# Dense passes of a two-layer attention and mixture kernel spread over three places, and layer 1's gates by tanh in pieces

## The chip, the cores and the metric

One core of a Trainium2 chip runs the whole program. The metric is the device time of one execution in microseconds. TensorE (PE) multiplies, VectorE (DVE), ScalarE (ACT) and GpSimd (POOL) do the rest; SyncE (SP) issues most of the DMAs and runs, as every engine does, its instructions in order.

## The reference

x is 16 sequences of 256 rows of 128 numbers (4096 rows, 32 tiles of 128 rows). Two layers follow each other:

```python
xn = layernorm(x);  s = attention0(xn);  g = silu(mixture0(xn));  x = x + s * g
xn = layernorm(x);  s = attention1(xn);  g = silu(mixture1(xn));  x = x + s * g
```

Attention 0 is softmax attention of 16 heads with a relative bias; attention 1 works over channels (8 heads of 16 by 16, RMS norm, l2-normalised q and k). Mixture 0 has 8 experts (128 to 512 to 128, exact gelu), top 2, plus half a shared expert, and a layer norm with gamma and beta. Mixture 1 has 4 experts and top 2 by a router with a hidden layer of 256:

```python
rh = gelu(x @ rW1 + rb1); probs = softmax(rh @ rW2 + rb2)
w, idx = top_k(probs, 2)
out = sum_e combine_w[e] * (gelu(x @ We1[e] + be1[e]) @ We2[e] + be2[e])
```

## The kernel before

Everything is fp32 but the scores' operands. The rows chosen for an expert are scattered to DRAM by POOL (`scatter_rows`), loaded as tiles of 256 rows, multiplied, and scattered back by POOL (`store_outputs`, L803) to `yg_dram`; the two choices of each row are then fetched by SP (`fetch`, L621) into `yy` and added by DVE (`add_choices`, L2122).

A tile, on TensorE: `transposes`, `up_rows` (L1053, eight matmuls at L1057 into two of four banks), four gelus on ScalarE (`gelus`, L1465), `down_rows` (L1062, sixteen matmuls at L1068), and on DVE `outputs` (L2054: row numbers and weights at L2063 and L2064, add the bias at L2068, weigh at L2071). Layer 0 has NJ0 = 40 such tiles; layer 1 has NJ1 = 29, three of them half tiles (`LONELY`). Tiles are pipelined by one on TensorE; there are four weight buffers (`wb`), and SP loads weights and rows of tile j when those of tile j - 4 are free.

The first three sequences of layer 1 (6 tiles of rows, `TD`) aren't routed: each goes through all four experts, which makes twelve **dense passes** (`NDJ` = ND * E1) of one up and one down each; `keep_dense` (L2161, DVE) adds the bias and keeps the result, and `weigh_dense` (L2166) weighs and sums them later, beside tiles 4 to 7 of layer 1. Ten of the passes (`NDA`) run on TensorE after the last tile of layer 0, with eight **turns** of layer 1's router between them (`TURN`): a turn is `router_logits(b - 1)`, `router_hidden(b)` and `transpose_normalised(b + 3)` for the first eight sequences. ScalarE follows in the same order (`gelus`, `hidden`, `transposed_again`, `normalised`).

Beside these passes the second half of layer 0's output is finished: SP fetches it in two chunks of 8 tiles (`CHUNKS`), DVE adds (L2126), adds the shared part (L2135), takes statistics (L1610) and finishes them (`finish_half`, L2143), ScalarE normalises (`normalise_gate`, L1506), DVE applies gamma and beta (L2152, L2153), ScalarE takes the silu (L1515), DVE gates and adds to x (`add_gated`, L2158, L2159) and takes the statistics of the new x. Then ScalarE normalises sequences 8 to 15 (L1349), and the router runs on these. The other two passes stand after it, around `route_pe` (L881), two matmuls whose result DVE needs for the slots (`route_keep_counts`, L1746).

Then come attention 1, on TensorE, DVE and ScalarE, with POOL scattering rows beside it, and the 29 routed tiles. MID1 = 19 and MID2 = 25 part the rows, so that rows 0 to 11, 12 to 18 and 19 to 24 can be fetched during the last tiles (NJB = 19, NJC = 25; SP waits in `stored_through`, L625, until POOL's stores have landed). The tail: `silu(1, q)` on ScalarE, `gate_and_add` on DVE (L2324, L2325), the last rows fetched (25 to 31), added and gated, and five output DMAs (L672), which stand in SP's queue behind the last fetch.

## Time and profile before

| | |
|---|---|
| median of 3 runs | 760.46 us (759.81 to 763.92) |
| the profiled execution | 761.59 us |
| its span, first to last instruction | 759.8 us |
| mean granted TensorE clock | 0.981 of full speed |
| TensorE busy | 680.9 us, 90% |
| DVE busy | 543.9 us, 72% |
| ScalarE busy | 477.1 us, 63% |
| POOL busy | 435.5 us, 57% |
| between the layers: from TensorE's last matmul of layer 0 to its first transposition of sequence 8 | 487.2 to 541.5 us |
| routed tiles of layer 1 on TensorE | 630.8 to 740.1 us |

A busy share is an average over stages with different limits. What a change in a stage is worth is read in that stage: which instruction ends last, and what it waited for. Times in a timeline are microseconds from the start of the span; a row may merge several instructions of one group, and its second number is the time from the first one's start to the last one's end.

### The profile page before, as it was taken

How to read it: one execution, taken by the hardware profiler on the slowest of the kernel's cores; microseconds unless marked ns; L12 is line 12 of the kernel's file. 1: busy time of each engine (PE TensorE's matmuls, PEld its weight loads, DVE VectorE, ACT ScalarE, POOL GpSimd, SP SyncE). 2: the span in 40 equal slices, each digit the busy share in tenths (PEclk: the TensorE clock that was granted, in tenths of full speed). 3: DMA queues.
4: the chain of work that ended last, by engine and by line, in shares of the span. 5: the costliest groups of instructions: out<-in, count | busy, mean ns of one | idle time of the engine just before them, and what ended most of it. 6: DMA issues, size and time to landing. Idle time of an engine off the chain costs nothing. (4 is left out here: it accounts for less than half of the span.)

```text
span 759.8 us, 17184 instructions
## 1 busy us (share of the span) xinstructions
PE 680.9 (90%) x5393; PEld 475.5 (63%) x5393; DVE 543.9 (72%) x1277; ACT 477.1 (63%) x926; POOL 435.5 (57%) x393
## 2 busy tenths in 40 slices
PE   3887888999999999999999999799999898999890
PEld 2751333333333333379999888798888687989780
DVE  6889999999999999943333477664659893643356
ACT  4774677788888888864444648569652464544451
POOL 6912456899999999945555445400007767544452
PEclk9997999999999999999999999999999999999996
DMA  7975542223323233277888877450001523888865
GB/s 237 314 204 170 174 123 68 76 76 93 99 84 91 77 102 87 76 211 234 260 282 261 280 234 229 127 143 0 3 1 47 178 72 103 235 245 242 267 207 173
DMA packets 96462, 117.46 MB, mean 155 GB/s; under 512 B 10552, under 2 KB 72296, under 8 KB 96408
## 3 DMA queue, kind: packets, MB, share of 16 engines
q1 hardware_dynamic: 88376, 100.22, 45.0%
q0 software_dynamic: 8032, 16.58, 6.3%
q8 instruction: 26, 0.43, 0.2%
q14 instruction: 28, 0.23, 0.1%
HBM read 82.30 MB, written 34.32 MB: 153 GB/s over the span
## 5 line engine op out<-in xcount | busy, mean ns | idle before, releaser
L1473 ACT ACTIVATE work<-wide,work 128x256 f32<-128x256 f32 (+1 forms) x324 | 131.1, 469 | 133.5 <-PE wide L1057 132.4
L811 POOL DMA_INDIRECT yg_dram<-work x135 | 133.3, 987 | 135.7 <-DVE work L2071 108.8
L1634 DVE TENSOR_REDUCE work<-wide 128x4 bf16<-128x1024 f32 x128 | 154.4, 1224 | 8.2 <-PE wide L919 7.6
L1068 PE MATMUL wide<-work 128*128 128x128 f32 x1272 | 155.0, 275 | 0.4 <-ACT work L1473 0.4
L1068 PEld LDWEIGHTS wide<-work 128*128 128x128 f32 x1272 | 148.9, 192 | 1.6 <-ACT work L1473 0.8
L1057 PE MATMUL wide<-xT,work 128*128 128x256 f32 (+1 forms) x552 | 129.3, 377 | 7.4 <-issue 5.4
L1057 PEld LDWEIGHTS wide<-xT,work 128*128 128x128 f32 x552 | 98.1, 190 | 20.1 <-issue 8.0
L772 POOL TENSOR_TENSOR work<-work,biasT 128x1024 f32<-128x1024 f32 x30 | 71.1, 2372 | 39.9 <-ACT work L1402 39.3
L772 POOL TENSOR_TENSOR yy<-yy,biasT 128x1024 f32<-128x1024 f32 x30 | 71.2, 2372 | 17.4 <-ACT yy L1402 16.7
L919 PE MATMUL wide<-biasA,turnb 128*128 128x512 bf16 x256 | 80.0, 395 | 0.0
L1411 ACT ACTIVATE yy<-yy 128x1024 f32<-128x1024 f32 x64 | 67.4, 1055 | 18.8 <-DVE yy L1944 17.9
L2068 DVE TENSOR_TENSOR work<-wide,work 128x256 f32<-128x256 f32 x69 | 28.9, 419 | 66.6 <-PE wide L1068 65.8
L2039 DVE COPY xT<-wide 128x256 f32<-128x256 f32 x69 | 28.8, 417 | 66.7 <-PE wide L1079 65.9
L1411 ACT ACTIVATE work<-work 128x1024 f32<-128x1024 f32 x64 | 67.3, 1055 | 8.5 <-DVE work L1944 7.0
L764 POOL DMA_INDIRECT xg_dram<-bufB,sloti x64 | 63.3, 989 | 13.1 <-issue 12.0
L764 POOL DMA_INDIRECT xg_dram<-bufC,sloti x52 | 50.3, 968 | 19.3 <-issue 13.7
L957 PE MATMUL wide<-work 49*128 49x256 bf16 x512 | 50.8, 277 | 7.2 <-DVE work L1634 6.0
L915 PE MATMUL wide<-work 48*128 48x256 bf16 x512 | 50.9, 277 | 4.0 <-DVE work L1647 1.5
L957 PEld LDWEIGHTS wide<-work 49*128 49x128 bf16 x512 | 14.7, 94 | 50.4 <-issue 29.3
L974 PE MATMUL wide<-yy,work 128*25 128x256 f32 x512 | 41.0, 387 | 5.3 <-ACT yy L1411 4.4
L760 POOL TENSOR_SCALAR bufC<-tokf 128x13 f32<-128x13 f32 (+1 forms) x3 | 1.0, 345 | 77.2 <-DVE rt L1752 74.3
L974 PE MATMUL wide<-work 128*25 128x256 f32 x512 | 41.6, 398 | 1.0 <-ACT work L1411 0.7
(311 smaller groups left out, 1157.2 us busy)
## 6 DMA issues: line engine op xcount, KB each, us to landing
work<-in_wcat SPq DMA_DIRECT2D x73, 578.0 KB, 4.6
xg_dram<-empty SPq DMA_DIRECT2D x35, 260.0 KB, 2.8
work<-xg_dram SPq DMA_DIRECT2D x66, 130.0 KB
stk_dram<-yy SPq DMA_DIRECT2D x16, 384.0 KB, 3.2
work<-stk_dram SPq DMA_DIRECT2D x64, 96.0 KB
work<-stk_dram SPq DMA_DIRECT2D x64, 64.0 KB
yy<-yg_dram SPq DMA_DIRECT2D x8, 512.0 KB, 6.6
biasT<-ext_dram SPq DMA_DIRECT2D x8, 384.0 KB
```

The costliest lines, as they stand in the source:

```text
L764: g.indirect_dma_start(out=xg_dram[l], out_offset=bass.IndirectOffsetOnAxis(ap=sloti[k][:, t:t + 1].bitcast(u32), axis=0), in_=xn_sb[l][:, ...
L772: g.tensor_tensor(sc, sc, bass.AP(tensor=bt.tensor, offset=bt.offset + S - 1, ap=[list(bt.ap)[0], [4 * BW, 2], [P, 2], [-1, S]]), ALU.add) ...
L811: g.indirect_dma_start(out=yg_dram[l], out_offset=bass.IndirectOffsetOnAxis(ap=yid[v][:, s_:s_ + 1].bitcast(u32), axis=0), in_=yb[v][:, s_ ...
L915: mm(into[:, (2 * e + c) * S:(2 * e + c + 1) * S], qst[u][pair_rows(e, TROWS), place(t), qt * P:(qt + 1) * P], kst[u][pair_rows(e, TROWS), ...
L919: last = mm(into[:, e * 2 * S:(e + 1) * 2 * S], turnb[:, :], bass.AP(tensor=b_.tensor, offset=b_.offset, ap=[list(b_.ap)[0], [P, 2], [1, S]]),
L957: last = mm(wide[at][:, (2 * e + k) * S:(2 * e + k + 1) * S], kst[u][pair_rows(e), place(t), k * P:(k + 1) * P], qst[u][pair_rows(e), plac ...
L974: last = mm(PO[32 * i:32 * i + VCOLS, 0:S], vaug[u][:, k, h // 2, lo:lo + VCOLS], scores[t % NSC][:, at:at + S], start=(gr % 2 == 0 and k ...
L1057: last = mm(HP[u][c // 2][:, (c % 2) * TS:(c % 2) * TS + n * P], wb[v][:, c * P:(c + 1) * P], rows, start=True, stop=True)
L1068: last = mm(YP[u][:, s_ * D:(s_ + 1) * D], hb[u][:, c, s_ * P:(s_ + 1) * P], wb[v][:, HID + c * D:HID + (c + 1) * D], start=(c == 0), stop ...
L1411: A(scores[t], scores[t], ACT.Exp).then_inc(a["E"], 1)
L1473: A(hb[u][:, c, 0:n * P], bank[2 + 2 * u + c // 2][:, (c % 2) * TS:(c % 2) * TS + n * P], ACT.Gelu, bias=wb[v][:, bc:bc + 1]).then_inc(m[" ...
L1634: V.tensor_reduce(nmax[:, :, 2 * place(t):2 * place(t) + 2].rearrange("p c e -> p e c"), into[:, :].rearrange("p (e c k) -> p e c k", e=2, ...
```

## The change

The twelve dense passes are listed in `PASSES` and `LATE`: six (sequence 1's four, two of sequence 2's) stand between the layers, three (sequence 2's other two, and expert 0 of sequence 0) beside the second routing, and three (experts 1 to 3 of sequence 0) behind the last routed tile, with weight loads of their own on SP. The eight router turns are spread over six passes (`TURNED`). The bias of sequence 0's experts is loaded to `late_b2` early; DVE starts the sum of tiles 0 and 1 with the biases (`start_late`) and adds each late pass straight from PSUM (`weigh_late`). Layer 1's gate silu(z) * s becomes (tanh(z/2) + 1) * (0.5 * z * s), in six pieces (`GATES`), three DVE passes each with the addition (`gate_start`, `gate_scale`, `gate_add`) instead of two; pieces 0 and 1 are finished beside the last routed tiles, and their output DMAs stand earlier in SP's queue. DVE waits for POOL's last scatter before piece 2. The second half of layer 0's output comes in three chunks, all fetched ahead of the fourth expert's weights; DVE normalises one quarter of it and ScalarE the other, before gelu 4; the two silus stand behind the passes, between two explicit table loads. `weigh_dense` covers tiles 2 to 5. The bodies that only pass other ranges (`take_stats`, `add_shared`, `gate_stats`, `row_stats`) and the like are left out of the diff.

```diff
-OUT_PARTS = ((0, 12), (12, 19), (19, 25), (25, 29), (29, T))
-CHUNKS = (((0, 8), (8, 16), (16, 24), (24, T)), ((0, 12), (12, 19), (19, 25), (25, T)))
-GATED = ((0,), (1,), (2,), (3, 4))
+OUT_PARTS = ((2, 6), (6, 12), (12, 19), (19, 25), (0, 2), (25, 29), (29, T))
+CHUNKS = (((0, 8), (8, 16), (16, 20), (20, 24), (24, T)), ((0, 12), (12, 19), (19, 25), (25, T)))
+GATES = ((2, 6), (6, 12), (12, 19), (19, 25), (0, 2), (25, T))
 MID1, MID2 = 19, 25
...
 STACK_ROUNDS = (5, 6, 10, 11, 12, 13, 14, 15)
-TURN = {0: 0, 1: 1, 2: 2, 3: 3, 5: 4, 6: 5, 7: 6, 8: 7}
+TURNED = ((0,), (1,), (2, 3), (4,), (5, 6), (7,))
 TD = ND * S // P
-NDJ = ND * E1
-NDA = NDJ - 2
+PASSES = tuple((b, e) for b in (1, 2) for e in range(E1)) + ((0, 0),)
+LATE = ((0, 1), (0, 2), (0, 3))
+NDJ = len(PASSES)
+NDA = len(TURNED)
+LAST_PASS = [max(j for j in range(NDJ) if j % 4 == v) for v in range(4)]
+assert all(e == j % 4 for j, (_, e) in enumerate(PASSES))
 
 
...
                     load_weights(1, 1)
+                    sp.dma_start(late_b2, bass.AP(tensor=wcat1.tensor, offset=wcat1.offset + WROW - D,
+                                                  ap=[[WROW, P], [P * WROW, E1], [1, D]])).then_inc(s_bt, 16)
...
+                    if l and j == NJC + 1:
+                        store_part(0)
...
+                            for q in range(2, 5):
+                                fetch(q, 0)
+                                fetch(q, 1)
                         sp.dma_start(wb[e], wcat1[e * P:(e + 1) * P, :]).then_inc(moe[1][f"W{e}"], 16)
-                    fetch(3, 0)
-                    fetch(3, 1)
...
+                    for j, (_, e) in enumerate(LATE, nj):
+                        sp.wait_ge(m["yb"], j + (1 - NWB))
+                        sp.dma_start(wb[j % NWB], wcat1[e * P:(e + 1) * P, :]).then_inc(m[f"W{j % NWB}"], 16)
+                    store_part(1)
                     stored_through(nj)
                     for k in range(TOPK):
                         fetch(3, k)
...
+            for i in range(2, len(OUT_PARTS)):
+                store_part(i)
...
+            pool.sem_inc(com[1]["sent"], 1)
...
+            def late_passes():
+                m = moe[1]
+                for k, (b, _) in enumerate(LATE):
+                    j = NJ1 + k
+                    pe.wait_ge(m[f"W{j % NWB}"], j // NWB * 16 + 32)
+                    up_rows(m, j + NDJ, j % NWB, xTd[b])
+                    if k:
+                        down_rows(m, j - 1 + NDJ, (j - 1) % NWB)
+                down_rows(m, NJ1 + len(LATE) - 1 + NDJ, (NJ1 + len(LATE) - 1) % NWB)
...
+            def router_turn(b):
+                pe.wait_ge(pre[1]["xT"], min(b + 2, NB // 2 - 1) + 3)
+                if b:
+                    router_logits(b - 1, (b - 1) % 2)
+                router_hidden(b, b % 2)
+                if b + 3 < NB // 2:
+                    transpose_normalised(b + 3)
...
+                pe.wait_ge(pre[1]["xT"], PASSES[j][0] + 3)
+                up_rows(m, j, v, xTd[PASSES[j][0]])
+                router_turn(TURNED[j][0])
...
-                if j in TURN and TURN[j] + 3 < NB // 2:
-                    transpose_normalised(TURN[j] + 3)
+                for b in TURNED[j][1:]:
+                    router_turn(b)
+            router_logits(NB // 2 - 1, 1)
             down_rows(m, NDA - 1, (NDA - 1) % NWB)
             pe.wait_ge(m["gelu"], NDA * 4 + 8)
             pe.wait_ge(pre[1]["lg"], 2 + 1)
             staged([(transpose_normalised, 1), (router_hidden, 2), (router_logits, 3)], NB // 2, NB)
             pe.wait_ge(pre[1]["lg"], 2 + 2)
-            for j in (NDA, NDA + 1):
-                up_rows(m, j, j % NWB, xTd[j // E1])
-            down_rows(m, NDA, NDA % NWB)
+            for j in range(NDA, NDJ):
+                up_rows(m, j, j % NWB, xTd[PASSES[j][0]])
+                if j > NDA:
+                    down_rows(m, j - 1, (j - 1) % NWB)
+            route_pe(1, E1, bank[0], bank[1])
+            down_rows(m, NDJ - 1, (NDJ - 1) % NWB)
...
-            route_pe(1, E1, bank[0], bank[1])
-            down_rows(m, NDA + 1, (NDA + 1) % NWB)
...
+                for j in range((SPANS[-1][0] if l else LOOPED[0]) * NWB, nj):
+                    if l and j == SPANS[-1][0] * NWB:
+                        half_tanh(0)
                     gelus(m, j + DENSE[l], j % NWB, j // NWB * 16 + (32 if l else 16))
                     if l == 0:
                         beside_experts(j)
...
+                        half_tanh(1)
+
...
+
             experts(0, NJ0)
-            staged([(normalised, 0), (transposed_again, 1)], 0, ND)
-            normalised(ND)
+            staged([(normalised, 0), (transposed_again, 1)], 0, 3)
+            normalised(3)
             for j in range(NDA):
+                if j == 4:
+                    normalise_gate(3)
...
+                for b in TURNED[j]:
...
                     if b + 3 < NB // 2:
...
                     if b + 4 < NB // 2:
                         normalised(b + 4)
-                if j in (4, 5):
-                    normalise_gate(j - 2)
-                elif j == 6:
-                    silu(0, 2)
-                    silu(0, 3)
+            load_table(ACT.Silu, 0)
+            silu(0, 2)
+            silu(0, 3)
+            load_table(ACT.Gelu, 1)
             staged([(normalised, 0), (transposed_again, 1), (hidden, 2)], NB // 2, NB)
             route_act(1, E1)
-            for j in (NDA, NDA + 1):
+            for j in range(NDA, NDJ):
                 gelus(moe[1], j, j % NWB, 16)
 
...
             staged([(exponents, 2), (copy_product, 3), (scale_product, 4)])
...
-            for q in range(4):
-                silu(1, q)
+            half_tanh(2)
+            late_gelus(0)
+            half_tanh(3)
+            late_gelus(1)
+            late_gelus(2)
+            half_tanh(4)
+            half_tanh(5)
 
 
...
+                    if l and j == NJC + 2:
+                        gate_scale(1)
+                    elif l and j == NJC + 3:
+                        gate_add(1)
...
+                    elif j == NWB + E1:
+                        start_late((0, 1))
+                    elif j == NWB + E1 + 1:
+                        start_late((2, 3))
+                    elif j == NFULL + 5:
+                        gate_start(0)
+                    elif j == SPANS[-1][0] * NWB + 1:
+                        gate_scale(0)
+                    elif j == SPANS[-1][0] * NWB + 2:
+                        gate_add(0)
                     elif j in (NJB + 5, NJB + 7):
                         add_choices(1, (j - NJB - 5) // 2)
+                    elif j == NJB + 6:
+                        gate_start(1)
+                    elif j == NJC + 2:
+                        gate_start(2)
                     elif j == NJC + 3:
                         add_choices(1, 2)
 
             def beside_experts(j):
...
+            def normalise_third():
+                dve.wait_ge(com[0]["stats"], 2)
+                for t in range(16, 24):
+                    z = yy[:, 0, t, :]
+                    st.did(V.tensor_scalar(z, z, mean[:, t:t + 1], rstd[:, t:t + 1], ALU.subtract, ALU.mult))
+                st.sync()
 
             def finish_half(h, done):
                 lo, hi = h * T // 2, (h + 1) * T // 2
...
+                    dve.sem_inc(com[1]["z"], 1)
+
+            def gate_start(i):
+
+                lo, hi = GATES[i]
+                dve.wait_ge(com[1]["z"], i + 1)
+                st.link(V.scalar_tensor_tensor(s_sb[:, lo:hi, :], yy[:, 0, lo:hi, :], 0.5, s_sb[:, lo:hi, :], ALU.mult, ALU.mult))
+
+            def gate_scale(i, part=None):
+                dve.wait_ge(com[1]["silu"], i + 1)
+                lo, hi = GATES[i] if part is None else OUT_PARTS[part]
+                st.link(V.scalar_tensor_tensor(yy[:, 1, lo:hi, :], yy[:, 1, lo:hi, :], 1.0, s_sb[:, lo:hi, :], ALU.add, ALU.mult))
+
+            def gate_add(part):
+                lo, hi = OUT_PARTS[part]
+                V.tensor_tensor(yy[:, 0, lo:hi, :], xres[:, lo:hi, :], yy[:, 1, lo:hi, :], ALU.add).then_inc(com[1]["x1"], 1)
+
+            def start_late(experts_):
+
+                for e in experts_:
+                    for t in range(2):
+                        weight = cw[:, t * E1 + e:t * E1 + e + 1]
+                        z = yy[:, 0, t, :]
+                        if e:
+                            st.did(V.scalar_tensor_tensor(z, late_b2[:, e, :], weight, z, ALU.mult, ALU.add))
+                        else:
+                            st.did(V.tensor_scalar(z, z, weight, None, ALU.mult))
+                    st.sync()
+
+            def weigh_late(k):
+                j, e = NJ1 + k + NDJ, LATE[k][1]
+                dve.wait_ge(moe[1]["down"], j + 3)
+                dve.wait_ge(moe[1]["y"], j + 4)
+                for t in range(2):
+                    z = yy[:, 0, t, :]
+                    ins = V.scalar_tensor_tensor(z, bank[6 + (NJ1 + k) % NWB % 2][:, t * D:(t + 1) * D],
+                                                 cw[:, t * E1 + e:t * E1 + e + 1], z, ALU.mult, ALU.add)
+                ins.then_inc(moe[1]["y"], 1)
+                if k == len(LATE) - 1:
+                    dve.wait_ge(moe[1]["y"], j + 5)
+                    dve.sem_inc(com[1]["z"], 1)
 
             experts(0, NJ0)
-            add_choices(0, 2)
-            add_shared(2)
-            gate_stats(2)
-            keep_dense(0)
-            add_choices(0, 3)
-            add_shared(3)
-            gate_stats(3)
-            keep_dense(1)
+            for q in (2, 3, 4):
+                lo, hi = CHUNKS[0][q]
+                add_choices(0, q)
+                add_shared(lo, hi)
+                gate_stats(lo, hi)
+                if q > 2:
+                    keep_dense(q - 3)
             finish_half(1, com[0]["stats"])
-            for j in range(2, 5):
-                keep_dense(j)
+            normalise_third()
             gamma_beta(2)
+            keep_dense(2)
+            gamma_beta(3)
+            keep_dense(3)
+            add_gated(2)
+            row_stats(16, 24)
+            add_gated(3)
+            row_stats(24, T)
+            finish_half(1, com[0]["x1"])
+            router_logits(0)
+            keep_dense(4)
             keep_dense(5)
-            gamma_beta(3)
-            keep_dense(6)
-            add_gated(2)
-            add_gated(3)
-            row_stats(2)
-            keep_dense(7)
-            row_stats(3)
-            finish_half(1, com[0]["x1"])
-            keep_dense(8)
...
             route_weights(1)
+            keep_dense(NDA)
             route_keep_counts(1, bank[0], bank[1])
             route_sums(1)
             route_blocks()
             route_places_second()
...
-
+            for j in range(NDA + 1, NDJ):
+                keep_dense(j)
 
             def next_rows(b, u, turn):
...
+            gate_add(2)
+            weigh_late(0)
+            gate_start(3)
+            gate_scale(3)
+            gate_add(3)
+            weigh_late(1)
+            weigh_late(2)
+            gate_start(4)
+            gate_scale(4)
+            gate_add(4)
             add_choices(1, 3)
-            gate_and_add(3)
+            last = len(GATES) - 1
+            gate_start(last)
+            for part in (last, last + 1):
+                gate_scale(last, part)
+                gate_add(part)
 
 
 # ---- launch: one core; layouts only ----
```

## Rows read from the trace of the kernel before

**Rows 1.** timeline of TensorE, 512 to 519: start us, us, engine line op out<-in xcount.

```profile
512.21 1.89 PE L1057 MATMUL wide<-biasA,work 128*128 128x256 f32 x8
513.93 0.95 PE L1158 MATMUL wide<-packed,rh 128*128 128x4 f32 x8
514.75 1.11 PE L1149 MATMUL wide<-biasA,packed 128*128 128x256 f32 x4
515.69 1.95 PE L1068 MATMUL wide<-work 128*128 128x128 f32 x16
517.69 1.89 PE L1057 MATMUL wide<-biasA,work 128*128 128x256 f32 x8
```

**Rows 2.** timeline of the handover, all engines; brackets: idle before, and releaser.

```profile
505.20 1.23 DVE L2126 TENSOR_TENSOR yy<-yy 128x1024 f32<-128x1024 f32 x1 [0.27 <-DMA yy<-yg_dram]
...
512.55 3.19 ACT L1509 ACTIVATE yy<-yy,shift,rstd 128x128 f32<-128x128 f32 x8 [1.06 <-DVE shift L2146]
...
523.53 1.28 ACT L1515 ACT_TABLE_LOAD   x1
...
524.82 2.25 ACT L1515 ACTIVATE yy<-yy 128x1024 f32<-128x1024 f32 x2
...
528.78 1.21 DVE L2158 TENSOR_TENSOR yy<-yy,bufA 128x1024 f32<-128x1024 f32 x1
...
540.11 0.17 DVE L2146 SCALAR_TENSOR_TENSOR shift<-mean,rstd 128x16 f32<-128x16 f32 x1
...
541.49 0.96 PE L1142 MATMUL wide<-ident,bufC 128*128 128x128 f32 x4 [0.69 <-DVE lg L1675]
```

**Rows 3.** windows: us, busy time of PE, PEld, DVE, ACT, POOL, PEclk, DMA.

```profile
58.00:59.00 1.00, 1.00 (x9) 0.27 (x9) 0.90 (x2) 0.89 (x3) 0.00 (x0) 0.84 0.19 59
65.00:66.00 1.00, 1.00 (x10) 0.31 (x8) 0.30 (x2) 0.48 (x1) 0.34 (x1) 0.75 0.00 0
744.00:746.00 2.00, 0.00 (x0) 0.00 (x0) 2.00 (x2) 0.00 (x0) 1.70 (x2) 0.69 0.10 33
```

**Rows 4.** timeline of TensorE near 72 and 79, the same eight matmuls.

```profile
72.25 1.04 PE L974 MATMUL wide<-work 128*25 128x256 f32 x8
...
79.50 0.63 PE L974 MATMUL wide<-work 128*25 128x256 f32 x8
```

**Rows 5.** timeline of the second routing, 558 to 568.

```profile
558.41 3.72 PE L1057 MATMUL wide<-biasA,work 128*128 128x256 f32 x16 [0.32 <-DVE lg L1675]
...
562.56 2.05 PE L1068 MATMUL wide<-work 128*128 128x128 f32 x16 [0.43 <-ACT work L1473]
...
565.29 0.47 PE L885 MATMUL wide<-rt,below 128*128 128x104 f32 x2 [0.46 <-DVE rt L1732]
...
566.09 0.27 DVE L1750 COPY rt<-wide 128x104 f32<-128x104 f32 x1 [0.59 <-PE wide L886]
...
567.62 1.06 PE L1208 MATMUL wide<-biasT 128*128 128x128 f32 x8
```

**Rows 6.** timeline of the loop over routed tiles, 661 to 667.

```profile
661.79 1.66 DVE L2174 SCALAR_TENSOR_TENSOR yy<-yy,cw 128x128 f32<-128x128 f32 x6
...
666.22 0.44 PE L1079 MATMUL wide<-ident,work 128*128 128x128 f32 x2 [0.75 <-DMA work<-xg_dram]
```

**Rows 7.** timeline of the tail, 731 to the end.

```profile
731.98 1.70 ACT L1473 ACTIVATE work<-wide,work 128x256 f32<-128x256 f32 x4 [2.03 <-PE wide L1057]
...
739.99 0.96 POOL L811 DMA_INDIRECT yg_dram<-work  x1 [1.17 <-DVE work L2064]
740.14 0.42 DVE L2068 TENSOR_TENSOR work<-wide,work 128x256 f32<-128x256 f32 x1 [0.75 <-PE wide L1068]
...
744.70 1.49 POOL L811 DMA_INDIRECT yg_dram<-work  x1 [0.30 <-issue]
...
752.73 1.09 DVE L2126 TENSOR_TENSOR yy<-yy 128x896 f32<-128x896 f32 x1 [3.38 <-DMA yy<-yg_dram]
...
756.75 0.56 DVE L2325 TENSOR_TENSOR yy<-bufB,yy 128x384 f32<-128x384 f32 x1
```

121 lines of the change are left out of this document (53 added, 68 removed).

## The prediction

> **What bounds the kernel now.** I read the page first (TensorE busy 90% of a 759.8 us span), then the busy time in windows, then the timeline of four stretches that the change touches: the handover between the layers, the second routing, the loop over the routed tiles of layer 1, and the tail. The chain of waits names what ends last in each. In the handover (about 487 to 541 us) two chains run side by side and end together. TensorE never rests: ten dense passes and eight router turns, start to start without a hole. An up takes 1.72 us (512.21 to 513.93), logits 0.82, a hidden product 0.94, a down with a transposition 2.0; a pass alone is 3.52, a pass with a turn 5.48 (512.21 to 517.69), so a turn is 1.96 [rows 1]. Beside it, the second half of layer 0's combine: DVE adds the last fetched chunk from 505.20, ScalarE normalises from 512.55, the two silus end at 527.07, DVE multiplies and adds from 528.78 and has the row statistics at 540.29; TensorE restarts at 541.49 [rows 2]. In the second routing (558.4 to 567.6) TensorE's two passes surround two counting matmuls, on which DVE's slot computation waits [rows 5]. In the expert loop TensorE is full, with small stalls [rows 6]. In the tail TensorE is done at 740.1, and the time is last rows stored, fetched, added, gated, sent out [rows 7].
>
> **The change, part by part** (times are those of the profiled execution, moved).
>
> *Handover.* Six passes are left and two turns share a pass twice. From up(3)'s old start at 503.2 the third pass carries one more turn: up(3) 505.2, up(4) 510.6, up(5) 510.6 + 5.48 + 1.96, less 0.2 for transposes no longer there = 517.9. TensorE loses 4 x 3.52 = 14.1 us of work. But the x1 chain does not get shorter by that. DVE: the last half is fetched in three chunks ahead of the fourth weight load. Before, DVE waited for the last chunk until 505.20 [rows 2]; with 2.1 MB queued without the 0.6 MB of weights between, I take the last chunk as added from 503.8 (between 502 and 505.2). The last chunk has eight tiles as the second had before, so from its start to ScalarE's start is 512.55 - 505.20 = 7.35 us again: statistics at 511.2. ScalarE has its eight normalisations (3.19 us) now ahead of gelu 4: 511.4 to 514.6, so gelu 4 ends at 516.2 and the router's hidden 5 at 517.0, where TensorE wanted it at 515.9: a stall of 1.1 us. The other eight go to DVE (8 x 0.28 = 2.2 us, by six such in 1.66 us [rows 6]), which then needs two passes of 1.23 us a quarter for gamma and beta; z is ready at 516 and 518.9, not late for anybody. The silus stand behind hidden 7 in ScalarE's queue. Hidden 7: up(5) at 519.0 with the stall, 1.8 + 0.8 + 1.0 us more on TensorE, 0.85 on ScalarE: 523.6. Then a 1.28 us table load [rows 2] with its small activation, 0.2: 525.1, first silu 1.13 (half of the two): 526.3. From there the chain is the old one: 540.29 - 528.78 = 11.5 us [rows 2], less 0.4 for the keep_dense that stood in it: 537.4. The logits of the first half are now kept before the last two keep_dense, so TensorE restarts one ScalarE normalisation and a transposition wait later, 0.95 us, at 538.4: **3.1 us earlier** (1.5 to 5).
>
> *The gap it opens.* TensorE is done with pass 5 at 522.7 + 1.75 + 0.8 + 1.85 = 527.1 and has nothing until 538.4: 11.3 us. Before, this gap was 0.7 us [rows 2]. In the tail, TensorE ended at 740.1 and the granted clock fell from 1.00 to 0.50 within 744 to 746 [rows 3]; so here it is at 1.2 GHz from about 531.5. How long it stays there once work is back: near the start it fell within 58 to 59 and came back within 65 to 66, 6.7 us, with TensorE working nearly all of them [rows 3]. Between none and these I take 5 us, nearer to the only row. Eight matmuls of L974 span 1.04 us there and 0.63 us at 2.4 GHz, a factor of 1.65 that includes fixed latencies [rows 4]; I take 1.9 for the stream. The second half of the router (541.49 to 558, eight sequences) keeps TensorE and ScalarE both busy all the time, so nothing is caught up: 5 x (1 - 1/1.9) = **2.4 us lost** (0 to 3.8).
>
> *Second routing.* Three passes instead of two. Now two ups from 558.41, down 6 from 562.56 behind the gelu table load, up 8 at 564.4, down 7 at 566.1, and only then, at 567.9, the counting matmuls that ran at 565.29 and for which DVE was ready at 565.24 [rows 5]. DVE's copy of the counts moves from 566.09 to 568.6. TensorE's first gram matmul moves from 567.62 to 568.4 + 1.8 + 0.3 = 570.5 [rows 5], and the attention of layer 1 starts on that and runs at DVE's pace with no slack to return it: **2.9 us lost** (2.5 to 3.5). POOL's scatters start 2.5 us later, but the rows they give are loaded long before TensorE asks.
>
> *Loop over routed tiles.* weigh_dense does 4 tiles instead of 6 in each of four turns: 1.66 us becomes 1.1. It stands in the one chain in which DVE's ids, SP's row load and TensorE's 0.75 us stall follow each other [rows 6]: **0.5 us gained** (0 to 0.75). start_late, the gate pieces of 4 and 6 tiles and the tanh of 0.6 and 0.8 us fit in DVE's gaps of a microsecond and in ScalarE's 2.03 us a tile [rows 7]; the 256 KB of late_b2 and the two early output parts ride in SP's queue, at about 0.4 us an issue, where nobody waits (0 to 1 each, in the range). Two places don't fit: gate_scale(1) and gate_add(1) stand before the last two tiles' outputs. An elementwise pass costs 1.09 us at 896 columns and 0.56 at 384 [rows 7], so by the straight line 1.23 at 1024, 0.96 at 768, 0.69 at 512, 0.43 at 256. gate_add(1) follows gate_start(2), ends at 741.3, and the last tile's y comes at 742.4 instead of 741.0.
>
> *Tail.* The last y is 1.4 us later, but POOL was behind anyway: its last scatter began at 744.70 and took 1.49 us while DVE ran big passes, where an undisturbed one takes 0.96 [rows 7]. The new wait on "sent" holds DVE back until POOL is done, at about 745.8, so the fetch goes out at 747.1 instead of 747.5. Queued on DVE behind that wait are, in order: gate 2 (2.2 us, to 748.0), weigh_late(0) 0.6, gate 3 (3 x 0.96, to 751.5), weigh_late(1) and (2) 1.3, gate 4 (3 x 0.4, to 754.1), and only then the last add, which before began at 752.73 when the fetch landed [rows 7]. The three late passes need 3 x 3.52 = 10.6 us of TensorE from 740.1: done at 750.8, hidden behind DVE. From the last add: 1.1 + 1.1 (gate_start on 7 tiles, tanh beside it) + 2 x 0.69 + 2 x 0.56 + 0.1 = 4.7 us: 758.8 against 757.31 before: **1.5 us lost** (gain 1 to loss 3). The output behind it is the same four and three tiles.
>
> Sum: -3.1 + 2.4 + 2.9 - 0.5 + 1.5 = **+3.2 us**. The profiled execution took 761.59 us (span 759.8 and 1.8 around it), so 764.8; the median of the runs is 1.1 lower, 760.46, so **763.7 us**. A measurement of this kernel tells about 0.5% (3.8 us) from no change: faster is below 756.7, slower above 764.3.
>
> **The rivals.**
> (1) *No slow clock.* The gap is shorter, or the clock comes back at once. Against it is the fall 4.5 us after the end of work [rows 3]. 761.3 us.
> (2) *Table loads, the slower side.* Tanh may not lie in the table that Gelu uses. Then each tanh among the gelus costs ScalarE two loads of 1.28 us [rows 2]. In the loop the extra 3.2 to 3.4 us exceed the 2.03 us of idle by 1.2 to 1.4, which the next tile's idle takes up. In the tail it decides as soon as DVE reaches weigh_late(1) before TensorE's pass is done: two loads between late gelus 0 and 1 put the last down at 752.1, and a further exposed load follows it; 0.7 to 2.6 us, I take 1.5: 765.2 us. No row shows a tanh, for or against. The Trainium skill, "ScalarE: Activation LUTs", section on table sets, lists tanh beside exp and beside sigmoid but not beside gelu. The same page gives 2.66 us for a switch, with a drain behind the load; by that two more exposed switches would make it some 768. The trace disagrees: the silu at 524.82 starts 0.01 us after the load [rows 2].
> (3) *The handover follows DVE alone, the faster side.* If ScalarE came to the silus when z is ready (518.9) instead of behind hidden 7, x1 would be there at 519.0 + 11.1 = 530.1, TensorE would restart at 531.1 and the gap of 4 us would hardly touch the clock: -10.4 + 2.9 - 0.5 + 1.5 = -6.5, 754.0 us. Against it: ScalarE runs in order, and five turns of TensorE stand before that point. It decides if passes and turns together take a seventh less than the rows say.
> (4) *More queueing than I see* in the tail or the second routing (late weights of 0.6 MB each land in the same stretch as the last fetch), each at the upper end of its range: 768 us.
>
> **How the numbers follow.** Forecast 0.47, its own range 761.5 to 766; no slow clock 0.12; table loads 0.15; faster handover 0.15; more queueing 0.11. Faster: rival 3 and a little, 0.16. Slower: 0.4 of the forecast, most of rivals 2 and 4: 0.38. Same: 0.46. Likeliest 763.7. The range of 757 to 768.5 leaves out most of rival 3 below and the end of rival 4 above.
>
> **What would show it.** In the changed profile: TensorE idle for about 11 us before the transpositions of sequence 8, with granted clock 0.50 in the windows after about 4 us of it, and the restart near 538. Counting matmuls 2.6 us later after the last logits than before (6.9 us), first gram 12.1 us after them instead of 9.2. No stall near tile 9. No table load among the gelus of the loop. DVE without a pause between the wait on "sent" and the last add, and the last add later than its fetch. Wrong would be: silus starting right when z is ready, a gap under 5 us, the last add waiting for its DMA, or the chain of waits ending in TensorE's late passes.

## Result and profile after

The kernel after took 764.7 us, median of 20 runs (762.06 to 779.8); the kernel before, beside it on the same chip, 761.3 us. The ratio is 1.0038, 95% interval 1.0025 to 1.0051: slower by 2.9 us (1.9 to 3.9), under the 0.5% that the prediction set as its bound for a change of the time. (The prediction's own mark for slower, 764.3 us, was counted from a median of 3 runs, 760.46; the 20 runs give 761.3.) The ratio leaves out the one run of 779.8 us, in which the granted clock was lower throughout (0.95 on average, 0.97 to 0.98 in the others). Forecast were 763.7 us and +3.2 us.

The profiled execution of after took 762.06 us (span 760.3), the fastest of its runs, so that beside the 761.59 us of before it shows only 0.5 us of the loss. So the time is compared stretch by stretch, between fixed points. A second profile was taken of either kernel (`before_look` and `again`, below); this table has all four, in us, from marks in the timelines of TensorE and DVE. The first row is a moment, and each other row is the time from the mark above it:

| stretch | before | before_look | after | again |
|---|---|---|---|---|
| TensorE's first transposition of layer 1 begins (a moment) | 487.19 | 486.70 | 486.00 | 488.24 |
| from there to TensorE's restart (sequence 8) | 54.30 | 54.30 | 50.35 | 50.59 |
| to DVE's reading of the last logits | 16.64 | 16.63 | 18.87 | 18.50 |
| to the first gram matmul | 9.49 | 9.76 | 13.22 | 13.23 |
| to the first routed tile of layer 1 | 63.16 | 63.00 | 62.78 | 62.80 |
| to the end of TensorE's last routed tile | 109.32 | 108.59 | 109.03 | 108.19 |
| to DVE's last instruction | 17.21 | 16.91 | 17.52 | 17.52 |

The means give -3.8 (handover), +2.05 (router), +3.6 (second routing), -0.3 (attention), -0.35 (routed tiles), +0.5 (tail): +1.7 us, where the ratio says +2.9. Two profiles of a kernel are few. Ten more come from the experiments below, each of which leaves most of these stretches as they are in after. Taken over all profiles in which the code of a stretch is that of after, with the kernel before in its two, the means are:

| stretch | profiles | mean (range) | against before |
|---|---|---|---|
| handover | 6 | 50.7 (50.4 to 51.0) | -3.6 |
| router | 6 | 18.6 (18.5 to 18.9) | +2.0 |
| second routing | 4 | 13.5 (13.2 to 14.5) | +3.9 |
| attention | 5 | 62.7 (62.5 to 62.8) | -0.35 |
| routed tiles | 10 | 109.1 (107.7 to 110.3) | +0.1 |
| tail | 8 | 18.1 (17.4 to 19.4) | +1.0 |

These add up to +3.1 us, which agrees with the ratio. The start of layer 1 scatters as well, from 486.0 to 489.3 us, in code that the change doesn't touch.

TensorE and DVE in the page of after, busy time and share:

```profile
PE 682.1 (90%) x5393; PEld 478.4 (63%) x5393; DVE 553.6 (73%) x1300; ACT 473.5 (62%) x921; POOL 434.1 (57%) x393
```

DVE has 10 us more work than before (543.9), TensorE about the same (680.9 before); neither says where the time went. The timeline of the handover, which answers to [rows 2] (start, us, engine, line, operation; brackets: idle before, and releaser):

```profile
502.29 1.23 DVE L2197 TENSOR_TENSOR yy<-yy 128x1024 f32<-128x1024 f32 x1 [0.26 <-DMA yy<-yg_dram]
...
509.65 3.19 ACT L1548 ACTIVATE yy<-yy,shift,rstd 128x128 f32<-128x128 f32 x8 [0.86 <-DVE shift L2224]
...
515.14 1.03 PE L1187 MATMUL wide<-packed,rh 128*128 128x4 f32 x8 [0.23 <-ACT rh L1394]
...
521.52 1.28 ACT L1558 ACT_TABLE_LOAD   x1
...
522.92 1.99 ACT L1554 ACTIVATE yy<-yy 128x1024 f32<-128x1024 f32 x2
524.00 1.23 DVE L2237 TENSOR_TENSOR yy<-yy,bufA 128x1024 f32<-128x1024 f32 x1 [6.62 <-ACT yy L1554]
...
535.22 1.65 ACT L1382 ACTIVATE bufC<-bufB,shift,rstd 128x128 f32<-128x128 f32 x4 [8.79 <-DVE shift L2224]
536.35 1.26 PE L1171 MATMUL wide<-ident,bufC 128*128 128x128 f32 x4 [11.27 <-ACT bufC L1382]
```

DVE adds the last chunk at 502.29 (before 505.20), and ScalarE's normalisation follows at 509.65, as DVE's does. DVE waits 6.62 us for the first silu, which stands in ScalarE's queue behind the turns; that is the price of silus behind the passes. Then TensorE waits 11.27 us for the new x (0.69 before). The windows of the two stretches in which the granted clock fell (busy time of PE, PEld, DVE, ACT, POOL; PEclk; DMA):

```profile
524.00:528.00 4.00, 1.09 (x10) 0.90 (x9) 3.93 (x10) 2.40 (x3) 0.00 (x0) 1.00 0.01 2
528.00:530.00 2.00, 0.00 (x0) 0.00 (x0) 1.97 (x3) 0.00 (x0) 0.00 (x0) 0.53 0.00 0
530.00:536.00 6.00, 0.00 (x0) 0.00 (x0) 5.55 (x30) 0.78 (x2) 0.00 (x0) 0.50 0.00 0
536.00:538.00 2.00, 1.65 (x5) 1.08 (x6) 1.69 (x10) 1.82 (x6) 0.00 (x0) 0.50 0.00 0
541.00:542.00 1.00, 1.00 (x7) 0.85 (x5) 0.00 (x0) 0.74 (x3) 0.00 (x0) 0.61 0.00 0
542.00:543.00 1.00, 1.00 (x10) 0.97 (x10) 0.00 (x0) 1.00 (x4) 0.00 (x0) 1.00 0.00 0
...
555.00:556.00 1.00, 0.68 (x3) 0.59 (x3) 0.72 (x3) 0.37 (x1) 0.00 (x0) 0.72 0.00 0
556.00:558.00 2.00, 2.00 (x6) 1.56 (x5) 1.49 (x6) 0.64 (x2) 0.00 (x0) 0.50 0.04 8
558.00:559.00 1.00, 1.00 (x4) 0.80 (x4) 0.90 (x4) 0.99 (x2) 0.00 (x0) 0.58 0.00 0
```

TensorE runs at 1.2 GHz from 528.1 on and for 5.4 us behind its restart, and again from 555.4 to 558.8 (a granted clock of 0.50 is 1.2 GHz, one of 1.00 is 2.4; the moments are worked out from the means of the windows). The profile of before shows 1.00 in every window from 524 to 574. The timeline of the second routing, which answers to [rows 5]:

```profile
555.49 5.36 PE L1076 MATMUL wide<-biasA,work 128*128 128x256 f32 x16 [0.32 <-DVE lg L1728]
...
560.69 1.95 PE L1087 MATMUL wide<-work 128*128 128x128 f32 x16
...
562.48 1.89 PE L1076 MATMUL wide<-biasA,work 128*128 128x256 f32 x8
...
564.21 1.95 PE L1087 MATMUL wide<-work 128*128 128x128 f32 x16
...
565.99 0.37 PE L904 MATMUL wide<-rt,below 128*128 128x104 f32 x2
...
566.62 0.27 DVE L1803 COPY rt<-wide 128x104 f32<-128x104 f32 x1 [3.44 <-PE wide L905]
```

DVE now waits 3.44 us for the counting matmuls (0.59 before). The chain of waits in the tail (start, us, what), and the instructions of DVE and POOL on which the prediction's tail rested:

```profile
740.25 3.64 PE wide L1076 x16
743.89 1.78 PE wide L1087 x16
745.67 1.73 PE wide L1076 x8
747.40 3.59 PE wide L1087 x32
750.99 0.02 issue
751.01 0.62 DVE yy L2295 x2
```

```profile
743.27 0.96 POOL L829 DMA_INDIRECT yg_dram<-work  x1 [0.79 <-DVE work L2124]
...
743.55 1.09 DVE L2271 SCALAR_TENSOR_TENSOR yy<-yy,bufA 128x896 f32<-128x896 f32 x1 [0.16 <-POOLq L852]
...
744.54 0.96 POOL L829 DMA_INDIRECT yg_dram<-work  x1 [0.30 <-issue]
...
751.01 0.61 DVE L2295 SCALAR_TENSOR_TENSOR yy<-wide,cw,yy 128x128 f32<-128x128 f32 x2 [1.18 <-PE wide L1087]
...
753.05 1.08 DVE L2197 TENSOR_TENSOR yy<-yy 128x896 f32<-128x896 f32 x1
...
757.21 0.56 DVE L2275 TENSOR_TENSOR yy<-bufB,yy 128x384 f32<-128x384 f32 x1
```

The wait on "sent" (L2271's) holds DVE for 0.16 us; it ends at 743.55, before the row of POOL's last scatter even begins (744.54). The tail hangs on TensorE's late passes; compare [rows 7], where it hung on the fetch.

### The profile page after: what moved, and what is told of

It is laid out like the page before. It is cut to its first block and busy times, and to the rows that moved or that the text cites. A ratio compares the mean times of both kernels' runs of the same rounds, so it can differ in the third digit from the quotient of the medians.

```text
span 760.3 us, 17196 instructions
## 1 busy us (share of the span) xinstructions
PE 682.1 (90%) x5393; PEld 478.4 (63%) x5393; DVE 553.6 (73%) x1300; ACT 473.5 (62%) x921; POOL 434.1 (57%) x393
## 5 line engine op out<-in xcount | busy, mean ns | idle before, releaser
L1506 ACT ACTIVATE work<-wide,work 128x256 f32<-128x256 f32 (+1 forms) x324 | 130.9, 468 | 137.7 <-PE wide L1076 136.7
L938 PE MATMUL wide<-biasA,turnb 128*128 128x512 bf16 x256 | 78.3, 388 | 0.0
L782 POOL DMA_INDIRECT xg_dram<-bufC,sloti x52 | 50.4, 969 | 19.3 <-issue 14.3
L976 PE MATMUL wide<-work 49*128 49x256 bf16 x512 | 50.7, 276 | 7.5 <-DVE work L1687 6.3
```

The costliest lines, as they stand in the source:

```text
L782: g.indirect_dma_start(out=xg_dram[l], out_offset=bass.IndirectOffsetOnAxis(ap=sloti[k][:, t:t + 1].bitcast(u32), axis=0), in_=xn_sb[l][:, ...
L938: last = mm(into[:, e * 2 * S:(e + 1) * 2 * S], turnb[:, :], bass.AP(tensor=b_.tensor, offset=b_.offset, ap=[list(b_.ap)[0], [P, 2], [1, S]]),
L976: last = mm(wide[at][:, (2 * e + k) * S:(2 * e + k + 1) * S], kst[u][pair_rows(e), place(t), k * P:(k + 1) * P], qst[u][pair_rows(e), plac ...
L1506: A(hb[u][:, c, 0:n * P], bank[2 + 2 * u + c // 2][:, (c % 2) * TS:(c % 2) * TS + n * P], ACT.Gelu, bias=wb[v][:, bc:bc + 1]).then_inc(m[" ...
```

## The experiments

Ratios are to the kernel before, run on the same chip; differences to after are differences of ratios with their intervals added as squares. Edits are against after, and `...` stands for lines left out.

**1. Fill the gap** (`gap_filled`). 44 wide matmuls that nobody reads, ahead of the wait for sequence 8:

```diff
+            for _ in range(44):
+                mm(bank[3], identb[:, :], bass.AP(tensor=identb[:, :].tensor, offset=identb[:, :].offset,
+                                                  ap=[list(identb[:, :].ap)[0], [0, 4], [1, P]]), start=True, stop=True)
             pe.wait_ge(pre[1]["lg"], 2 + 1)
```

> The changed kernel with 44 wide bf16 matmuls put on TensorE in the 11 us gap before the transpositions of sequence 8 (9.5 us of work, into a bank that nobody reads). Nothing else differs. If the slow clock after the gap costs what the prediction said, the median falls by 2.4 us against the changed kernel (764.7), to about 762.3, the granted clock stays at 1.00 from 525 to 555, and the second half of the router takes 16.6 us (as before) instead of 18.9. The rival, that the gap and its clock cost nothing because ScalarE paces that stretch, gives 764.7. A third outcome, that the filler delays the restart, would show as idle under 0.2 us before it and more than 764.7.

1.0042 (1.0023 to 1.0061), 764.3 us: no gain. The clock stayed at 1.00 to 539 us and then fell all the same, from 539.7 to 543.1, after 1.6 us of idle time and in the restart's first work, and again from 556.7 to 563.6. So the run didn't take the slow clock away, and it can't price it.

**2. Counting matmuls ahead of down 7** (`route_early`).

```diff
             for j in range(NDA, NDJ):
                 up_rows(m, j, j % NWB, xTd[PASSES[j][0]])
+                if j == NDJ - 1:
+                    route_pe(1, E1, bank[0], bank[1])
...
-            route_pe(1, E1, bank[0], bank[1])
```

> The changed kernel with the two counting matmuls moved between the up of the third pass beside the second routing and the downs that follow, so that DVE has its counts 1.8 us earlier, while TensorE does the same work in the same stretch. If TensorE's extra pass is what delays attention 1 (the prediction's reading), the first gram matmul stays where it is and the median changes by 0 to -0.5 us. The rival, that DVE's slot computation is what the attention waits for, gives -1.8 us.

1.0032 (1.0012 to 1.0051), 764.9 us: 0.5 us under after (interval -1.3 to +2.2), which alone doesn't exclude the rival's 1.8. The profile does. The counting matmuls came 9.0 us after the last logits (10.8 in after), but the first gram matmul 13.24 us after them, as in after (13.22): it stands behind both downs in TensorE's queue. What the third pass costs is TensorE's time, not DVE's wait for the counts.

**3. The late passes left out** (`no_late`): the sum of sequence 0 lacks experts 1 to 3. Their weight loads, gelus and other weighings go with them.

```diff
-            late_passes()
...
-            weigh_late(0)
...
-            weigh_late(1)
-            weigh_late(2)
```

> The changed kernel without the three dense passes behind the last routed tile, their weight loads, gelus and weighings (experts 1 to 3 of sequence 0 are left out of the sum). The prediction said the passes are hidden behind DVE, which costs 1.5 us in the tail; the trace of the changed kernel shows instead DVE waiting 1.18 us for the last pass. Without them DVE is free of 1.9 us of weighing and 1.2 us of wait, but the last add can't start before its rows have landed, about 752.7. So if the late passes cost what the changed trace shows beyond the fetch, -0.4 us; by the prediction's 1.5 us, -1.5 us; if the fetch itself is slowed by the late weight loads and the early outputs, more than that, up to -2.5 us.

1.0012 (0.9995 to 1.0029), 763.1 us: 2.0 us (0.4 to 3.6) under after. The tail took 16.53 us in its profile, 17.52 in after and 18.1 in the mean of eight profiles; its last add waited 2.17 us for the fetch, as it did in before (3.38). So all three late passes together, 10.7 us of TensorE's time, cost 1.0 to 1.6 us by the tail, and 0.4 to 3.6 by the runs.

**4. Two passes into the gap** (`gap_passes`): passes 6 and 7 follow pass 5 (NDB is 8), one is left beside the routing. Their gelus stand behind the silus, and two `keep_dense` move between DVE's last steps to the new x.

```diff
             router_logits(NB // 2 - 1, 1)
+            for j in range(NDA, NDB):
+                up_rows(m, j, j % NWB, xTd[PASSES[j][0]])
+                down_rows(m, j - 1, (j - 1) % NWB)
-            down_rows(m, NDA - 1, (NDA - 1) % NWB)
-            pe.wait_ge(m["gelu"], NDA * 4 + 8)
+            down_rows(m, NDB - 1, (NDB - 1) % NWB)
+            pe.wait_ge(m["gelu"], NDB * 4 + 8)
```

> The changed kernel with two of the three passes beside the second routing moved into the 11 us gap: up and down of passes 6 and 7 follow the router's last turn, their gelus stand behind the silus on ScalarE, and two keep_dense (0.4 us each, one of them inside the statistics chain) move with them. One pass is left beside the second routing. By the prediction's terms: the gap shrinks from 11.3 to about 4 us and the slow clock mostly goes (-1 to -2.4 us), the second routing loses two of its three passes (-2.9 to -4 us), the chain to the new x grows by 0.4. Sum -4 to -6 us: 759 to 761, below the kernel before. The rival, that the second routing is bound by DVE and not by the passes, gives -2 us; that the passes in the gap delay the restart, no gain at all.

1.0008 (0.9989 to 1.0027), 763.6 us: 2.3 us (0.5 to 4.1) under after, and no different from before. From the last logits to the first gram matmul it took 12.0 us, where the terms gave about 9: with only one pass there, TensorE waited 3.10 us for DVE, and the clock was at 0.50 from 557.5 to 571.2.

**5. Both kernels once more, for their profiles.**

> The kernel before, unchanged, for a second profile. If the second fall of TensorE's clock belongs to the change, this profile shows a granted clock of 1.00 from 524 to 574 us again, as the first one does, and the sixteen matmuls of two ups beside the second routing span 3.7 us. If it is a matter of the execution, the clock falls here too, and those sixteen span over 5 us.

> The kernel after, unchanged, for a second profile. I expect the fall of the clock in the 11 us gap (to 0.50 from about 528 to 542 us) and a second one in the second routing, of 3 to 13 us, between 555 and 571; the handover from TensorE's last matmul of layer 0 to its restart within 50.3 to 51.5 us, and the first gram matmul 12 to 14.5 us after the last logits were read. A theory in which the second fall is chance of one execution expects none in this one.

The slow clock in the second routing does not belong to the change. Windows of `before_look`, and the two ups in it:

```profile
559.00:560.00 1.00, 1.00 (x5) 0.80 (x4) 0.90 (x4) 0.86 (x1) 0.00 (x0) 0.61 0.00 0
560.00:562.00 2.00, 2.00 (x7) 1.55 (x6) 1.79 (x7) 1.99 (x5) 0.00 (x0) 0.50 0.00 0
562.00:563.00 1.00, 1.00 (x5) 0.86 (x4) 0.90 (x4) 0.73 (x3) 0.00 (x0) 0.69 0.00 0
...
557.91 5.41 PE L1057 MATMUL wide<-biasA,work 128*128 128x256 f32 x16 [0.32 <-DVE lg L1675]
```

The sixteen matmuls took 5.41 us instead of 3.72 [rows 5], and yet the first gram matmul came only 0.27 us later (9.76 against 9.49). `again` repeated after: the clock was at 0.50 from 529.9 to 543.5 and from 557.2 to 560.6, handover 50.6, routing 13.23. It took 763.35 us.

**6. Two passes beside the routing again** (`two_beside`): the ninth pass is left out, so the sum of sequence 0 lacks expert 0.

```diff
-            for j in range(NDA, NDJ):
+            for j in range(NDA, NDJ - 1):
                 up_rows(m, j, j % NWB, xTd[PASSES[j][0]])
...
```

> Leaves out the ninth dense pass (expert 0 of sequence 0), so the sum of the first two tiles lacks that expert, and two passes stand beside the second routing, as before the change. Prediction's term: the third pass costs 2.9 us there (2.5 to 3.5), so the median is 2.5 to 3.5 us under that of the kernel after, about 761.8, and the first gram matmul comes 9.5 to 10.5 us after the last logits are read where the kernel after shows 13.2. Rival: the delay of that stretch is the slow clock's and not the pass's; then the clock still falls there, the passes that are left run slowly for longer, and the median falls by under 1.5 us.

0.9991 (0.9973 to 1.0008), 759.9 us: 3.6 us (1.9 to 5.2) under after. The routing took 10.88 us where after has 13.22, though the clock fell for 6.8 us (555.3 to 562.1). By either measure (2.3 us of the stretch, 3.6 of the runs) the third pass is the largest single cost that was taken out on its own, and the prediction's 2.9 lies between them.

**7. Passes in the gap, and filling** (`gap_passes_fill`): as `gap_passes`, with

```diff
+            def logits_and_fill(b, u, turn=0):
+                router_logits(b, u)
+                fill({NB - 3: 1, NB - 2: 3, NB - 1: 2}.get(b, 0))
...
             pe.wait_ge(m["gelu"], NDB * 4 + 8)
+            fill(20)
```

> The two passes 6 and 7 moved from the second routing into the gap (as in gap_passes), with 20 wide matmuls of 16 bits behind them and 1, 3 and 2 such matmuls behind the logits of sequences 13, 14 and 15, whose results nobody reads. Theory: what is left of the loss is TensorE's slow clock, 6 us of it around the restart and 13 us in the second routing in gap_passes. If the filling keeps the clock at 1.00 in both places, the first gram matmul comes 8 to 9.5 us after the last logits and the median is 2 to 4 us under gap_passes, near 760, at or below the kernel before. Rival: the fall does not depend on what TensorE does there (or comes later all the same, as it did with the 44 fillers); then the median is that of gap_passes, 763.6, within 1 us, or above it by the fillers' own time.

1.0014 (0.9997 to 1.0030), 762.1 us, against 1.0008 without filling: no gain. The clock held through the restart (from ScalarE's first normalisation to the last logits 18.10 us, 19.62 in `gap_passes`, where it fell) and then fell from 562.4 to 569.2, late in a wait of 4.88 us of TensorE for DVE, with the first gram matmul at 12.0 us after the logits again.

**8. Eight, two and two passes** (`eight_two_two_fill`, `eight_two_two`): expert 1 of sequence 0 goes into that wait.

```diff
-PASSES = tuple((b, e) for b in (1, 2) for e in range(E1)) + ((0, 0),)
-LATE = ((0, 1), (0, 2), (0, 3))
+PASSES = tuple((b, e) for b in (1, 2) for e in range(E1)) + ((0, 0), (0, 1))
+LATE = ((0, 2), (0, 3))
```

> gap_passes_fill with one of the three late passes (expert 1 of sequence 0) moved beside the second routing, where TensorE waited 4.88 us for DVE in gap_passes_fill: eight passes between the layers, two beside the routing, two in the tail. Theory: a pass in that wait costs nothing, and the engine doesn't run slowly behind it, so the first gram matmul comes 9.5 to 10 us after the last logits (12.0 there); the tail is shorter by about 1.0 us, since it is bounded by TensorE's late passes down to DVE's own chain. Together 3.5 us under gap_passes_fill (762.07): 758.6, under the kernel before (761.5) by 3. Rival: the second pass delays the counting matmuls and only the tail's gain is left, 761.

> The same without the 26 wide matmuls that fill TensorE's pauses. Theory: what the filling is worth is the slow clock around the restart (restart to last logits 18.5 us in gap_passes against 16.4 with filling) and in the second routing, 2 to 4 us in all: about 761. Rival: the filling is worth nothing once two passes stand in the routing again; then it is within 0.7 us of the kernel with filling.

With filling 0.9969 (0.9954 to 0.9983), 759.95 us: 2.4 us under before (1.3 to 3.5) and 5.2 under after. It is the one version whose interval lies wholly under before, though by less than the 0.5% named above, and it is the best of the ten that were tried. The routing took 9.71 us, as expected. The tail did not get shorter than in after (17.57 us), because TensorE waits 1.89 us for the weights of the first late pass:

```profile
741.07 3.72 PE L1078 MATMUL wide<-biasA,work 128*128 128x256 f32 x16 [1.89 <-DMA work<-in_wcat]
```

Eight, two and two is not alone in this. With three late passes TensorE waited for late weights in five of the eight profiles of that tail (0.44, 0.46, 0.47, 0.98 and 1.78 us), and their tails took 18.1 to 19.4 us; in the three without a wait it was 17.4 to 17.5. The longest wait, in the profile of `after_fill` (experiment 10):

```profile
743.71 3.72 PE L1076 MATMUL wide<-biasA,work 128*128 128x256 f32 x16 [1.78 <-DMA work<-in_wcat]
```

Without filling 0.9984 (0.9968 to 1.0000), 760.8 us; its clock fell in both places (535.8 to 542.6, 556.2 to 559.7). The difference of 1.1 us (interval -0.6 to +2.8) is open.

**9. No wait on "sent"** (`no_sent`).

```diff
-            dve.wait_ge(com[1]["sent"], 1)
```

> The kernel after without DVE's wait for POOL's last scatter ahead of gate piece 2. The prediction had this wait hold DVE for over 1 us and set the tail; the trace of after shows it released at once (0.16 us) and the chain of waits in TensorE's late passes. If the trace tells the truth, the median is that of the kernel after, 764.7, within 0.7 us. If the wait costs what the prediction gave it, it falls by 1 us or more.

1.0038 (1.0025 to 1.0052), 765.0 us: no difference to after (0.0, 1.4 us to either side). A cost of the size that the prediction gave the wait, over 1 us, isn't seen. In its one profile POOL's last scatter took 1.82 us beside DVE's passes (0.96 in after) and the last add waited 0.69 us for the fetch, so the long scatter that the prediction feared can happen; one profile doesn't show what decides it.

**10. After with the clock held** (`after_fill`): `fill(50)` in the gap and the 1, 3 and 2 behind the logits, as in 7.

> The kernel after with 50 wide matmuls of 16 bits in the gap (44 in gap_filled, which ended 1.6 us before the restart) and 1, 3 and 2 behind the logits of sequences 13, 14 and 15; nothing else is changed. Theory: the slow clock costs after about 2 us at the restart (restart to last logits 18.5 to 18.9 us against 16.4 at full clock) and 1 to 2 us in the second routing. If the granted clock stays at 1.00 from 524 to 574 us, the restart comes where it did, the logits 2.2 us earlier and the routing 1 to 1.5 us shorter, and the median is 2 to 3.5 us under that of after: about 762. Rival: the attention behind these stretches runs at the pace of another engine, or the fillers delay the restart by what they give back; then the median is within 1 us of after, 764.7.

1.0016 (0.9997 to 1.0035), 763.5 us: 1.7 us under after (interval -0.1 to 3.4). This time the clock was 1.00 in every window from 524 to 574. The two that were slow in after:

```profile
541.00:543.00 2.00, 2.00 (x14) 1.60 (x12) 1.37 (x7) 1.82 (x6) 0.00 (x0) 1.00 0.00 0
557.00:559.00 2.00, 2.00 (x10) 1.77 (x11) 1.49 (x6) 1.22 (x2) 0.00 (x0) 1.00 0.00 0
```

From ScalarE's first normalisation of the new x to the last logits it took 18.11 us (20.00 in after and 19.63 in `again`, at the slow clock; 17.81 in before), and from there to the first gram matmul 12.27 (13.22). (I count from ScalarE here, since the fillers part the first transpositions into two groups.) What came ahead was longer by 0.8 us: ScalarE began 50.16 us after the first mark of the table, where after has 49.22 and `again` 49.46, and a row of DVE shows where, at the last chunk's fetch (1.28 us of wait, 0.26 in after):

```profile
505.56 1.23 DVE L2207 TENSOR_TENSOR yy<-yy 128x1024 f32<-128x1024 f32 x1 [1.28 <-DMA yy<-yg_dram]
```

That wait lies ahead of the fillers and is not theirs. Over the three pairs with and without filling in which it held the clock at the restart (this one, 7 and 8), the mean of the differences is -0.8 us, with an interval of about 1.0 to either side, which doesn't exclude zero.

## Why the prediction was right, and where it wasn't

*Handover, forecast -3.1.* Right in its mechanism, and near in its times: the last chunk from 502.3 (503.8 forecast), ScalarE's stall 0.2 us instead of 1.1, the gap 11.27 (11.3), the silus behind hidden 7, which settles the third rival (they did not start when z was ready). Measured from a fixed point of the same code it gave -3.8, and -3.6 over six profiles. The step that was too careful is hidden 5's stall. ScalarE's normalisations ended at 512.8, 1.8 us ahead of the forecast; 1.2 of that is this profile's early start of layer 1, and 0.6 are left. The statement that TensorE never rests in the handover of before isn't quite so: it waits for ScalarE, 1.30 us before 489.17 and 0.70 us before 530.83.

*Slow clock, forecast +2.4.* The clock fell, at 528 rather than 531.5, and came back 5.4 us after the restart (5 taken, between none and 6.7). The stretch to the last logits grew by 2.05 us. Holding the clock at 1.00 gave back 1.5 to 1.9 of them (18.1 us instead of 19.6 to 20.0), not all: 0.3 us against before are left, unexplained (the six wide matmuls among the logits stand in this stretch; their own time was not measured). So the factor of 1.9 over 5 us, 2.4 us, was too dear by 0.5 to 0.9. For the whole kernel the price is smaller than what the runs can tell: filling gained 1.7 us on after itself (-0.1 to 3.4) and 0.8 on the average of three pairs, and neither interval excludes zero. The first rival (no slow clock) didn't come.

*Second routing, forecast +2.9.* Measured +3.6 in two profiles, +3.9 in four. The third pass is right to within 0.1 us: with the clock held, the first gram matmul came 12.27 us after DVE's reading of the last logits (9.49 in before, so 2.8 more). The prediction's 570.5 is 12.4 on that scale; its 12.1 and 9.2 count from the first up, 0.28 us later. What was missing is a second fall of the clock right behind the router's narrow matmuls (four columns, sixteen in a row, and 0.3 us idle). It costs after 0.95 us (13.22 against 12.27), and it costs before 0.27, by one pair of profiles each: there TensorE has 0.43 us of wait for ScalarE and 0.46 for DVE in that stretch [rows 5], which the slow matmuls eat, and it has no third pass behind them. The prediction took the clock of this stretch from a single profile of before, which showed 1.00; the second profile of the same kernel showed 0.50. Its reason held: TensorE's own queue keeps the first gram matmul back, and not DVE's late counts (experiment 2).

*Routed tiles, forecast -0.5.* Not shown: -0.35 by two profiles each, +0.1 by ten against two, and the ten scatter by 2.6 us. The 0.75 us stall near 666 us, on which the term rested [rows 6], is gone in after, but the second profile of before doesn't show it either (0.37 us of wait for DVE there instead). It was not tested on its own.

*Tail, forecast +1.5.* Measured +0.5 in two profiles and +1.0 in eight, and the mechanism was wrong: the prediction had DVE as the bound and the late passes hidden, and named "the chain of waits ending in TensorE's late passes" as what would refute it. It ends there. The failed term is the wait on "sent", taken to 745.8 from a POOL scatter of 1.49 us in [rows 7]. The last scatters of after took 0.96 to 1.08 us, but that is the smaller part: the last one ends at 745.5 by its row. The larger part is that the wait was over at 743.55, ahead of that scatter and not behind it, in `again` too (744.85, with the last scatter from 745.83). So by these rows the wait does not hold DVE until POOL's last scatter is over, as the change meant it to. Without the wait the time is the same (experiment 9). DVE then has 1.18 us to spare before the last pass. TensorE's sum was right (750.8 forecast, 750.97 in the trace). The last add came at 753.05 instead of 754.1, and from there to the end it took 4.72 us (4.7 forecast). What lengthens the tail in other profiles is TensorE's wait for the late weights (experiment 8), which is the fourth rival, in a part: it was right that late weights can come into the way, and too dear at 768.

*Table loads (rival 2).* The timeline of ScalarE in after has a half-tanh (L1563) between gelus (L1506), without a load before or behind it:

```profile
735.94 1.62 ACT L1506 ACTIVATE work<-wide,work 128x256 f32<-128x256 f32 x4 [2.11 <-PE wide L1076]
737.45 0.95 ACT L1563 ACTIVATE yy<-yy 128x896 f32<-128x896 f32 x1
741.42 1.62 ACT L1506 ACTIVATE work<-wide,work 128x256 f32<-128x256 f32 x4 [3.02 <-PE wide L1076]
```

So it is with every half-tanh of the kernel, and the rival falls. The Trainium skill, "ScalarE: Activation LUTs", section on table sets, lists tanh beside exp and sigmoid and not beside gelu; this trace shows that the two can follow each other without a load.

The total was met (+3.2 against +2.9 by the ratio) because the terms' errors have both signs. By the larger set of profiles they are -0.5 in the handover, -0.4 at the clock, +1.0 in the routing, +0.6 in the routed tiles, -0.5 in the tail, and -0.35 in the attention, which the prediction left unchanged. That the sum came within 0.3 us of the ratio is luck in part: a fall of the clock that the prediction didn't have took the place of a wait that it had too long.

## What to carry over

Moving work into an engine's idle gap pays by what it stops delaying elsewhere: with the rest of the change as it is, the same twelve passes cost 2.9 us as six, three and three, and gained 2.4 us as eight, two and two with filling (1.2 without it, interval 0 to 2.4), since the two beside the routing fit into TensorE's waits there (0.43 and 0.68 us are left in `eight_two_two_fill`) and the third doesn't. Before pricing a moved pass, list for every stretch how long TensorE waits there for another engine; a pass costs only what exceeds it. Price also what the moved work brings with it: here its weights came to stand in the path of the tail. A clock seen at full speed in one profile is no fixed property of a stretch: take a second profile before leaving it out of the sum, and ask in which stretches a slow clock would be exposed.

## What the hardware showed that was not expected

- The granted clock fell to 0.50 at the second routing in ten of the eleven profiles that have no filling behind the logits (all but the first of before), for 3.4 to 13.6 us, always within 2 us of DVE's reading of the last logits; TensorE had run the router's matmuls of four columns just before. One, three and two wide matmuls among the last logits kept it at 1.00 through this point in three of three profiles.
- Filling a gap to within 1.6 us of the restart did not keep the clock (`gap_filled`: 0.50 from 539.7 to 543.1); filling it to the end did (three of three).
- Near tile 23 of layer 1 TensorE waits for a row load. In seven of the fourteen profiles this took 2.16 to 2.80 us, and the clock fell behind it in five of them; in the others it took at most 1.93 us, and the clock stayed. The row in after:

```profile
712.46 0.69 PE L1098 MATMUL wide<-ident,work 128*128 128x128 f32 x2 [2.19 <-DMA work<-xg_dram]
```

The clock was at 0.50 from 712.4 to 715.9 there. In the two profiles of before the wait at this tile was 1.36 and 1.60 us, and the clock stayed at 1.00. Why the load is late was not tried.
